# Layer 3 of a graph network: slots 1 to 11 as number pairs, blocks widened in five pieces, square roots placed later

## The chip, the cores and the metric

One NeuronCore of a Trainium2 chip runs the whole kernel. The metric is the device time of one execution in microseconds. TensorE multiplies, VectorE and ScalarE compute on vectors, GpSimd issues the gathers (indirect DMAs, which fetch rows by index), and SyncE issues the plain DMAs, of which ScalarE issues some too.

## The reference

Three graph convolutions over 6250 nodes and 106250 edges (100000 drawn ones, sorted by destination, and one self loop a node), then a residual and a layer norm:

```python
src = jnp.concatenate([edge_index[0], loops])
dst = jnp.concatenate([edge_index[1], loops])
deg = jax.ops.segment_sum(jnp.ones_like(dst, dtype=x.dtype), dst, num_segments=n)
dinv = jnp.where(deg > 0, jax.lax.rsqrt(deg), 0.0)
norm_edge = dinv[src] * dinv[dst]
for W, b in ((W1, b1), (W2, b2), (W3, b3)):
    h_in = h @ W
    agg = jax.ops.segment_sum(h_in[src] * norm_edge[:, None], dst, num_segments=n)
    h = jax.nn.relu(agg + b)
x = _layernorm(x + h, axis=-1)
```

Widths are 256 in, 512 hidden twice, 256 out. All is float32.

## The kernel before

The nodes are 49 tiles of 128. A layer's table (one row per node, already scaled by `dinv`) lies in DRAM, and each tile of the output is the sum of the rows that its edges name. The kernel has two ways to form such a sum, and layer 3 (`phase == 2`, from about 1900 us of the span on) uses both side by side.

**Gathered tiles.** The first 21 tiles (`GATHER`) of layer 3 take one *window* each. A window has up to 18 *slots*; a slot is 128 edges: GpSimd gathers their 128 source rows (L779), VectorE makes a 0/1 matrix `sel` from the destinations (L999, slots 0 to 8 "front" and 9 to 17 "back"), and TensorE multiplies the two into a PSUM sum. The window's sums alternate between `ps_acc` and `ps_d`. In layer 3 slots 1 to 8 (`PAIRED`) are fetched as *number pairs*: `table_pairs` holds each row as a high and a low part of type fp32r, 512 numbers or 2 KB, and TensorE multiplies `sel_r` with each part (L1743, two instructions of 256 columns). The other slots are fetched as single rows of 256 float32 numbers, 1 KB, and multiplied as float32 (L1747, which the trace shows as two instructions as well). Slots 0 and 9 to 17 are of that kind.

Rows are fetched into the place of the same slot of the window before. So GpSimd waits: slots 1 to 11 of window v are gathered as their groups were used in window v-1 (`slots_used`), and slots 12 to 15, and 16 and 17 where the tile needs them, after slot 0 of window v has been multiplied (`opened`), which shows that window v-1 is over.

**Dense tiles.** For the last 28 tiles (`DENSE`) the kernel has built matrices of counts earlier, 49 *blocks* of 128 by 128 to a tile, and stored them in DRAM, in bytes (`built_bytes`) or for ten of the tiles in bf16 (`built`). TensorE multiplies each block with the high and low parts of a source tile (L1850, 512 columns, fp32r), into `ps_T` and `ps_h` in turn. Before that, ScalarE *widens* the blocks to fp32r (L1526) from the loaded tile into one of two ring buffers, in pieces of 13 or 12 blocks (`PIECES`), 1664 or 1536 columns. After each piece ScalarE issues the load of the same piece of the tile after next (L1515). A widening waits until TensorE has finished the piece two before it (`dense_piece`), since it overwrites that ring buffer, and for the loaded tile (`blocks_in`).

**How they are interleaved.** Three windows and four dense tiles make a *group*; there are seven. TensorE's program is written out by hand: over the 54 slot positions of a group its 196 dense products are spread evenly, three or four of them ahead of each slot. Pieces are numbered 0 to 15 within a group, and four pieces are one tile.

**The square roots.** The layer norm of a finished tile runs on VectorE up to the variance (`mv`, L1100); ScalarE then takes the square root (`deviation`, L1534, which waits for `var_ready`), and VectorE goes on. ScalarE runs in order, so where `group` places a `deviation` among the widenings decides which piece waits behind it. A gathered tile is finished after its window's end: VectorE adds the sum (L1089), makes the next window's back half of `sel` and only then norms the tile. The names are `of_gather(g, b)` for window b and `of_dense(g, d)` for dense tile d of group g.

Of the kernel before, what the change touches and what calls it, by code (L numbers as in the profile page):

```python
# [30 lines left out]
P = 128  # L31
SLOTS = 18
FRONT = 9
PAIRED = range(1, FRONT)
GROUPS = [range(0, 1), range(1, 3), range(3, 6), range(6, 9), range(9, 12), range(12, 15), range(15, 16), range(16, 18)]
SURE = 16

STAY = 12
USED = 4
ORDER = [*range(0, SURE - 1), *range(SURE, SLOTS), SURE - 1]  # L40
# [21 lines left out]

PIECES = [(0, 13), (13, 25), (25, 37), (37, 49)]
LN_EPS = 1e-5


def gnn_program(nc, x, src, dst, W1, b1, W2, b2, W3, b3, out):
# [52 lines left out]
    with ctx:  # L120
# [52 lines left out]
        pair_rows = pair_rows_r.bitcast(F32)  # L173
        RING, RING_AT = PIECES[0][1], SINGLE + SLOTS * C
        ring = [rows_r[:, RING_AT + b * RING * P:RING_AT + (b + 1) * RING * P].rearrange("p (h d) -> p h d", d=P) for b in range(2)]
        assert PAIRED[0] == 1 and C + len(PAIRED) * 2 * C == SINGLE + (PAIRED[-1] + 1) * C and 2 * C == HID
        assert RING_AT + 2 * RING * P <= SLOTS * HID + COLS and all(hi_h - lo_h <= RING for lo_h, hi_h in PIECES)
        post = sb("post", [P, 2 * HID])
# [706 lines left out]
        def _(v_):  # L885
# [185 lines left out]
            def prepare_early(n, part, paired, to=sel):  # L1071

                if part == 0:
                    v_.wait_ge(slots_used, n * USED - 1)
                else:
                    v_.wait_ge(window_done, n)
                k = part * FRONT
                if paired and part == 0:
                    to = sel_r
                v.tensor_tensor(to[:, k:k + FRONT, :], numbers.unsqueeze(1).broadcast_to([P, FRONT, P]),  # L1080
                                early_dst[:, k:k + FRONT].unsqueeze(2).broadcast_to([P, FRONT, P]),
                                ALU.is_equal).then_inc((front_ready, back_ready)[part], 1)
# [28 lines left out]
            def finish_dense(g, d):  # L1111
                j, into, seq = DENSE_OF * g + d, d % 2, of_dense(g, d)
                v_.wait_ge(dense_piece, len(PIECES) * (j + 1))
# [65 lines left out]
            def one_window():  # L1179
                def steady(phase, t, odd, hots=None, whole=None, units=None, last=False, in_parts=False, tile=None, next_tile=None, dense=None):  # L1180
# [17 lines left out]
                    elif phase < 2:  # L1198
                        v.tensor_copy(idx[:, 1 - odd, :], early_src[:, :]).then_inc(idx_ready, 1)
                    prepare(n, t, base, 1, sel_parts if in_parts else sel)  # L1200
                    if phase == 1 and t > 1:
# [157 lines left out]
        def _(act):  # L1359
# [146 lines left out]
            def piece_in(j, into, piece):  # L1506

                lo_h, hi_h = PIECES[piece]
                its = blocks[into][:, lo_h:hi_h, :].rearrange("p h d -> p (h d)")
                return its.bitcast(U8)[:, 0:(hi_h - lo_h) * P] if in_bytes(j) else its  # L1510

            def load_blocks(j, into, piece):
                lo_h, hi_h = PIECES[piece]
                its = built_bytes if in_bytes(j) else built
                act.dma_start(piece_in(j, into, piece), its[j * P:(j + 1) * P, lo_h * P:hi_h * P]).then_inc(blocks_in[into], 16)  # L1515

            def widen(g, x, more=True):

                d, piece = divmod(x, len(PIECES))
                lo_h, hi_h = PIECES[piece]  # L1520
                whole_x = DENSE_OF * len(PIECES) * g + x
                act.wait_ge(blocks_in[d % 2], 16 * len(PIECES) * (DENSE_OF // 2 * g + d // 2 + 1))
                if not (isinstance(g, int) and whole_x < 2):
                    act.wait_ge(dense_piece, whole_x - 1)
                act.sem_inc(act_step, 1)
                nc.scalar.activation(ring[piece % 2][:, 0:hi_h - lo_h, :].rearrange("p h d -> p (h d)"),  # L1526
                                     piece_in(DENSE_OF * g + d, d % 2, piece), ACT.Copy).then_inc(widened, 1)
                if more:
                    act.wait_ge(widened, whole_x + 1)
                    load_blocks(DENSE_OF * g + d + 2, d % 2, piece)  # L1530
# [5 lines left out]
            def one_window():  # L1536
# [73 lines left out]
                act.wait_ge(tile_stored[1], 16 * len(PIECES) * (DENSE_1 // 2 + 2))  # L1610
                for piece in range(len(PIECES)):
                    load_blocks(0, 0, piece)
# [7 lines left out]
                for of in range(2):  # L1620
                    act.wait_ge(tile_stored[of], 16 * len(PIECES) * (DENSE // 2 + 1))
                for piece in range(len(PIECES)):
                    load_blocks(1, 1, piece)

                def group(g, first=False, last=False):

                    def pieces(*xs):
                        for x in xs:
                            widen(g, x, not (last and x >= 2 * len(PIECES)))

                    if not first:
                        deviation(of_gather(g - 1, 2))
                    if not first:
                        pieces(1)
                        deviation(of_dense(g - 1, 3))
                    pieces(2, 3, 4, 5)
                    deviation(of_dense(g, 0))
                    pieces(6)
                    deviation(of_gather(g, 0))
                    pieces(7, 8, 9)  # L1640
                    deviation(of_dense(g, 1))
# [31 lines left out]
        def _(pe):  # L1673
# [66 lines left out]
            def add_slot(to, phase, k, first, in_parts, start, stop):  # L1740
# [96 lines left out]
            def dense(g, d, h, first):  # L1837

                into = d % 2
                if h == 0:  # L1840
                    pe.wait_ge(dense_taken, DENSE_OF * g + d + 1)
                for piece, (lo_h, hi_h) in enumerate(PIECES):
                    if lo_h <= h < hi_h:
                        if h == lo_h:
                            pe.wait_ge(widened, len(PIECES) * (DENSE_OF * g + d) + piece + 1)
                        counts_of = ring[piece % 2][:, h - lo_h, :]
                        end = h == hi_h - 1
# [218 lines left out]
```

## Time and profile before

| | |
|---|---|
| time, median of 3 runs | 2373.16 us (2372.32 to 2376.5) |
| profiled execution: time | 2371.75 us |
| its span | 2369.9 us |
| TensorE busy | 2157.9 us, 91% of the span |
| GpSimd busy | 1696.4 us, 72% |
| VectorE, ScalarE busy | 866.9 us and 731.2 us |
| granted TensorE clock, mean | 0.978 |

The chain of work that ended last lies on TensorE for 56% of the span and on GpSimd for 14%. Times inside the trace are counted from the span's start. Shares over the whole span mix three layers with different limits; the change touches layer 3 alone.

### The profile page before, as it was taken

How to read it: one execution, taken by the hardware profiler on the slowest of the kernel's cores; microseconds unless marked ns; L12 is line 12 of the kernel's file. 1: busy time of each engine (PE TensorE's matmuls, PEld its weight loads, DVE VectorE, ACT ScalarE, POOL GpSimd, SP SyncE). 2: the span in 40 equal slices, each digit the busy share in tenths (PEclk: the TensorE clock that was granted, in tenths of full speed). 3: DMA queues.
4: the chain of work that ended last, by engine and by line, in shares of the span. 5: the costliest groups of instructions: out<-in, count | busy, mean ns of one | idle time of the engine just before them, and what ended most of it. 6: DMA issues, size and time to landing. Idle time of an engine off the chain costs nothing.

```text
span 2369.9 us, 33254 instructions
## 1 busy us (share of the span) xinstructions
PE 2157.9 (91%) x10765; PEld 1432.8 (60%) x10765; DVE 866.9 (37%) x1213; ACT 731.2 (31%) x1550; POOL 1696.4 (72%) x1768
## 2 busy tenths in 40 slices
PE   5777889999999998899998999989999899999998
PEld 4755567777777774444444444444444378888886
DVE  8887222222222212232333333333222334434333
ACT  7611223323333311232332323222231143443333
POOL 4277777777777766777777777777777777776774
PEclk9798999999999999999999999999999999999999
DMA  7446667677776766888887888888888787778884
GB/s 226 147 122 204 205 205 209 210 208 211 209 210 206 211 199 192 256 257 263 258 258 245 257 265 257 253 247 264 263 258 271 231 247 241 229 224 269 284 276 129
DMA packets 232394, 543.61 MB, mean 229 GB/s; under 512 B 39228, under 2 KB 107699, under 8 KB 232259
## 3 DMA queue, kind: packets, MB, share of 16 engines
q0 software_dynamic: 122592, 387.10, 55.1%
q1 hardware_dynamic: 91011, 121.92, 15.0%
q10 hardware_dynamic: 18656, 32.75, 4.3%
q8 instruction: 89, 1.46, 0.3%
q14 instruction: 46, 0.38, 0.1%
HBM read 455.62 MB, written 86.00 MB: 229 GB/s over the span
## 4 chain that ended last, share of the span: by engine, by line
PE 56%; POOL 14%; issue 13%; DMA 8%; DVE 7%; ACT 1%; POOLq 1%; ACTq 0%; DVEq 0%
POOL rows L779 14%; PE ps_o L1811 8%; PE ps_acc L1755 7%; PE ps_d L1755 7%; PE ps_h L1850 7%; DMA rows<-table,idx 7%; PE ps_d L1861 6%; PE ps_acc L1751 6%; PE ps_T L1850 5%; PE ps_h L1800 2%; PE ps_acc L1747 2%; PE ps_d L1747 2%; DVE big L942 1%; DMA rows<-table_parts,idx 1%; PE ps_e L1832 1%
## 5 line engine op out<-in xcount | busy, mean ns | idle before, releaser
L779 POOL DMA_INDIRECT rows<-table,idx x1081 | 1046.5, 968 | 374.9 <-issue 305.5
L1755 PE MATMUL ps_acc<-rows,sel 128*128 128x512 f32 (+2 forms) x1122 | 490.8, 566 | 81.1 <-DMA rows<-table,idx 58.6
L779 POOL DMA_INDIRECT rows<-table_parts,idx x483 | 456.6, 945 | 149.4 <-issue 139.5
L999 DVE SCALAR_TENSOR_TENSOR sel<-ps_e,firsts,dstT 128x1152 f32<-128x1152 f32 (+1 forms) x194 | 274.3, 1414 | 615.3 <-PE ps_acc L1755 209.1
L1755 PE MATMUL ps_d<-rows,sel 128*128 128x512 f32 (+1 forms) x850 | 411.3, 607 | 41.3 <-DMA rows<-table,idx 41.2
L1755 PEld LDWEIGHTS ps_acc<-rows,sel 128*128 128x128 f32 x1122 | 205.6, 201 | 231.2 <-issue 152.9
L1811 PE MATMUL ps_o<-low,hT 128*128 128x512 f32 (+1 forms) x784 | 272.2, 491 | 0.5 <-ACT hT L1433 0.5
L1751 PE MATMUL ps_acc<-rows,sel 128*128 128x256 bf16 (+1 forms) x1533 | 242.0, 274 | 23.1 <-DMA rows<-table_parts,idx 13.1
L1755 PEld LDWEIGHTS ps_d<-rows,sel 128*128 128x128 f32 x850 | 147.4, 191 | 178.5 <-issue 126.2
L1861 PE MATMUL ps_d<-big 128*128 128x256 bf16 x1470 | 226.6, 273 | 4.0 <-issue 3.6
L1850 PE MATMUL ps_T<-pairs_r,rows_r 128*128 128x512 f32 x686 | 210.1, 424 | 8.0 <-ACT rows_r L1526 8.0
L1811 PEld LDWEIGHTS ps_o<-low,hT 128*128 128x128 f32 x784 | 148.2, 193 | 104.9 <-issue 94.6
L1526 ACT ACTIVATE rows_r<-low 128x1664 fp32r<-128x1664 uint8 (+3 forms) x112 | 169.1, 1510 | 130.4 <-PE ps_h L1850 43.6
L1089 DVE TENSOR_TENSOR acc<-ps_acc,acc 128x256 f32<-128x256 f32 (+1 forms) x74 | 37.8, 511 | 464.0 <-PE ps_acc L1751 257.8
L1850 PE MATMUL ps_h<-pairs_r,rows_r 128*128 128x512 f32 x686 | 204.8, 418 | 2.6 <-ACT rows_r L1526 2.6
L779 POOL DMA_INDIRECT rows_r<-table_pairs,idx x168 | 159.0, 947 | 52.6 <-issue 48.7
L1454 ACT ACTIVATE big<-ps_o,dinv 128x256 f32<-128x256 f32 x49 | 23.2, 473 | 552.9 <-PE ps_o L1811 552.9
L1751 PEld LDWEIGHTS ps_acc<-rows,sel 128*128 128x128 bf16 x1533 | 148.2, 98 | 53.6 <-issue 17.9
L1861 PEld LDWEIGHTS ps_d<-big 128*128 128x128 bf16 x1470 | 140.2, 97 | 37.9 <-issue 25.6
L1850 PEld LDWEIGHTS ps_T<-pairs_r,rows_r 128*128 128x128 f32 x686 | 123.7, 189 | 29.9 <-ACT rows_r L1526 10.6
L1502 ACT ACTIVATE big<-ps_l 128x392 uint8<-128x392 f32 (+1 forms) x224 | 112.2, 501 | 95.2 <-PE ps_l L1832 94.9
L1850 PEld LDWEIGHTS ps_h<-pairs_r,rows_r 128*128 128x128 f32 x686 | 123.5, 189 | 25.0 <-issue 5.4
(215 smaller groups left out, 2084.0 us busy)
## 6 DMA issues: line engine op xcount, KB each, us to landing
rows<-table,idx POOLq DMA_INDIRECT x1081, 4.3
table<-made SPq DMA_DIRECT2D x49, 256.0 KB
acc<-table SPq DMA_DIRECT2D x49, 256.0 KB
table_pairs<-made_r SPq DMA_DIRECT2D x49, 256.0 KB, 4.3
built<-big SPq DMA_DIRECT2D x30, 384.0 KB
low<-built ACTq DMA_DIRECT2D x30, 384.0 KB, 4.8
built_bytes<-big SPq DMA_DIRECT2D x54, 192.0 KB
low<-built_bytes ACTq DMA_DIRECT2D x54, 192.0 KB, 3.9
```

What stands on the lines that cost most here:

```text
L779: pool.indirect_dma_start(out=to, out_offset=None, in_=its[0:nodes, :], in_offset=bass.IndirectOffsetOnAxis(ap=idx[:, of, k:k + 1], axis=0 ...
L999: v.scalar_tensor_tensor(to[:, k:k + FRONT, :], numbers.unsqueeze(1).broadcast_to([P, FRONT, P]), firsts[:, bass.ds(t, 1)], dstT[:, bass.d ...
L1089: v.tensor_tensor(acc[:, 0:w], ps[:, 0:w], acc[:, 0:w], ALU.add).then_inc(sum_taken, 1)
L1502: nc.scalar.activation(to[:, :, at:at + 2 * QUAD].rearrange("p h (b d) -> p h b d", b=2), built_banks[g % 2][:, 0:2 * QUADS].rearrange("p ...
L1526: nc.scalar.activation(ring[piece % 2][:, 0:hi_h - lo_h, :].rearrange("p h d -> p (h d)"), piece_in(DENSE_OF * g + d, d % 2, piece), ACT.C ...
L1747: return mm(to[:, 0:C], its, rows_3[:, k, :] if first is None else first, start=start, stop=stop)
L1751: ins = mm(to[:, 0:C], sel_parts[:, k, :], row[:, i * C:(i + 1) * C], start=start and i == 0, stop=stop and i == PARTS - 1)
L1755: return mm(to[:, 0:w], sel[:, k, :], rows_of[phase][:, k, 0:w] if first is None else first, start=start, stop=stop)
L1800: ins = mm(ps_h[:, m * P:(m + 1) * P], w1[:, k, m * P:(m + 1) * P], of[:, k * P:(k + 1) * P], start=(k == 0), stop=(k == KC - 1))
L1811: ins = mm(ps_o[:, 0:w], hT[:, m * P:(m + 1) * P], wt[:, m, :], start=(m == 0), stop=(m == KH - 1))
L1850: ins = mm(ps_dense[into].rearrange("p (i c) -> p i c", i=2), counts_of, pairs_r[:, :, h, :], start=(h == 0), stop=(h == T - 1))
L1861: ins = mm(ps_dense_1, making[of][:, h, :], parts[:, h, i, :], start=(h == 0 and i == 0), stop=(h == T - 1 and i == PARTS - 1))
```

## The change

It edits three things in layer 3. Slots 9, 10 and 11 are fetched and multiplied as number pairs too (`PAIRED` now ends at `STAY`, 12), and both halves of `sel` are made as `sel_r`. The widenings go by `RING_PIECES`, five pieces of 10, 10, 10, 10 and 9 blocks to a tile (1280 or 1152 columns), so that a group has 20 pieces; the ring index follows the running number of the piece, since five is odd. And `group` places the square roots elsewhere in the new order. The core of the diff:

```diff
-PAIRED = range(1, FRONT)
...
 STAY = 12
+PAIRED = range(1, STAY)
...
 PIECES = [(0, 13), (13, 25), (25, 37), (37, 49)]
+RING_PIECES = [(0, 10), (10, 20), (20, 30), (30, 40), (40, 49)]
...
-                if paired and part == 0:
+                if paired:
                     to = sel_r
...
-                    prepare(n, t, base, 1, sel_parts if in_parts else sel)
+                    prepare(n, t, base, 1, sel_parts if in_parts else sel_r if phase == 2 else sel)
...
-                nc.scalar.activation(ring[piece % 2][:, 0:hi_h - lo_h, :].rearrange("p h d -> p (h d)"),
+                nc.scalar.activation(ring[x % 2][:, 0:hi_h - lo_h, :].rearrange("p h d -> p (h d)"),
                                      piece_in(DENSE_OF * g + d, d % 2, piece), ACT.Copy).then_inc(widened, 1)
...
+                    if not first:
+                        pieces(1)
+                    pieces(2)
                     if not first:
                         deviation(of_gather(g - 1, 2))
+                    pieces(3)
                     if not first:
-                        pieces(1)
                         deviation(of_dense(g - 1, 3))
-                    pieces(2, 3, 4, 5)
+                    pieces(4, 5, 6)
                     deviation(of_dense(g, 0))
-                    pieces(6)
+                    pieces(7, 8)
                     deviation(of_gather(g, 0))
-                    pieces(7, 8, 9)
+                    pieces(9, 10, 11)
                     deviation(of_dense(g, 1))
-                    pieces(10, 11)
+                    pieces(12, 13, 14, 15)
                     deviation(of_gather(g, 1))
-                    pieces(12, 13, 14)
+                    pieces(16, 17, 18)
                     deviation(of_dense(g, 2))
-                    pieces(15)
+                    pieces(19)
...
                 if in_parts and phase == 2:
-                    its = sel_r[:, k, :].bitcast(F32) if k < FRONT else sel[:, k, :]
-                    return mm(to[:, 0:C], its, rows_3[:, k, :] if first is None else first, start=start, stop=stop)
+                    return mm(to[:, 0:C], sel_r[:, k, :].bitcast(F32), rows_3[:, k, :] if first is None else first, start=start, stop=stop)
...
-                        counts_of = ring[piece % 2][:, h - lo_h, :]
+                        counts_of = ring[(len(RING_PIECES) * d + piece) % 2][:, h - lo_h, :]
```

Everywhere else in layer 3 `PIECES` becomes `RING_PIECES`; the storing of the built blocks keeps the four old pieces. The number of instructions of GpSimd and VectorE does not change. Lines move by one to four: in the changed kernel L1747 is the product with a number pair (L1743 before), L1750 that with a single row (L1747 before), L1853 the dense product, L1527 the widening and L1535 the square root.

**ScalarE, the turn from group 0 to group 1.** `rows_r<-low` is a widening, `low<-built_bytes` the load behind it, `sd<-mv,eps` a square root. Before, from the widening of the new group's piece 0 on:

```order
L1526 ACTIVATE rows_r<-low 128x1664 [waits blocks_in0,dense_piece]
L1515 DMA low<-built_bytes 128x1664 [waits widened]
L1534 ACTIVATE sd<-mv,eps 128x1 [waits var_ready]
L1526 ACTIVATE rows_r<-low 128x1536 [waits blocks_in0,dense_piece]
L1515 DMA low<-built_bytes 128x1536 [waits widened]
L1534 ACTIVATE sd<-mv,eps 128x1 [waits var_ready]
L1526 ACTIVATE rows_r<-low 128x1536 [waits blocks_in0,dense_piece]
L1515 DMA low<-built_bytes 128x1536 [waits widened]
```

And now, from the same widening on:

```order
L1527 ACTIVATE rows_r<-low 128x1280 [waits blocks_in0,dense_piece]
L1516 DMA low<-built_bytes 128x1280 [waits widened]
L1527 ACTIVATE rows_r<-low 128x1280 [waits blocks_in0,dense_piece]
L1516 DMA low<-built_bytes 128x1280 [waits widened]
L1527 ACTIVATE rows_r<-low 128x1280 [waits blocks_in0,dense_piece]
L1516 DMA low<-built_bytes 128x1280 [waits widened]
L1535 ACTIVATE sd<-mv,eps 128x1 [waits var_ready]
L1527 ACTIVATE rows_r<-low 128x1280 [waits blocks_in0,dense_piece]
L1516 DMA low<-built_bytes 128x1280 [waits widened]
L1535 ACTIVATE sd<-mv,eps 128x1 [waits var_ready]
L1527 ACTIVATE rows_r<-low 128x1152 [waits blocks_in0,dense_piece]
L1516 DMA low<-built_bytes 128x1152 [waits widened]
```

The root of the last gathered tile stood ahead of piece 1 and now stands behind piece 2; the root of the last dense tile stood ahead of piece 2 and now stands behind piece 3.

**ScalarE, block 3 of group 0.** Before, the root of window 1's tile stands directly ahead of the first piece (1664 columns) of the fourth dense tile:

```order
L1526 ACTIVATE rows_r<-low 128x1536 [waits blocks_in0,dense_piece]
L1515 DMA low<-built_bytes 128x1536 [waits widened]
L1534 ACTIVATE sd<-mv,eps 128x1 [waits var_ready]
L1526 ACTIVATE rows_r<-low 128x1664 [waits blocks_in1,dense_piece]
L1515 DMA low<-built_bytes 128x1664 [waits widened]
```

Now, from the last piece (1152 columns) of the third dense tile on:

```order
L1527 ACTIVATE rows_r<-low 128x1152 [waits blocks_in0,dense_piece]
L1516 DMA low<-built_bytes 128x1152 [waits widened]
L1527 ACTIVATE rows_r<-low 128x1280 [waits blocks_in1,dense_piece]
L1516 DMA low<-built_bytes 128x1280 [waits widened]
L1535 ACTIVATE sd<-mv,eps 128x1 [waits var_ready]
L1527 ACTIVATE rows_r<-low 128x1280 [waits blocks_in1,dense_piece]
L1516 DMA low<-built_bytes 128x1280 [waits widened]
L1527 ACTIVATE rows_r<-low 128x1280 [waits blocks_in1,dense_piece]
```

The first piece of the fourth dense tile now comes ahead of that root, and its second piece behind it.

**TensorE, slots 9 and 10 of a window.** The rows are those of a steady window of layer 3, from the first of dense tile 2 (`ps_T`) on. Before:

```order
L1850 MATMUL ps_T<-pairs_r,rows_r 128x512 [waits widened,dense_taken]
L1850 MATMUL ps_T<-pairs_r,rows_r 128x512 x2
L1747 MATMUL ps_acc<-rows,sel 128x256 [waits back_ready,landed4]
L1850 MATMUL ps_T<-pairs_r,rows_r 128x512 x4
L1747 MATMUL ps_acc<-rows,sel 128x256
L1850 MATMUL ps_T<-pairs_r,rows_r 128x512 x3
```

And now:

```order
L1853 MATMUL ps_T<-pairs_r,rows_r 128x512 [waits widened,dense_taken]
L1853 MATMUL ps_T<-pairs_r,rows_r 128x512 x2
L1747 MATMUL ps_acc<-rows_r,sel_r 128x256 [waits back_ready,landed4]
L1747 MATMUL ps_acc<-rows_r,sel_r 128x256
L1853 MATMUL ps_T<-pairs_r,rows_r 128x512 x4
L1747 MATMUL ps_acc<-rows_r,sel_r 128x256 x2
L1853 MATMUL ps_T<-pairs_r,rows_r 128x512 x3
L1747 MATMUL ps_acc<-rows_r,sel_r 128x256 x2
```

Slots 9, 10 and 11 turn from `rows,sel` to `rows_r,sel_r`, with two products each where the order shows one; the dense products between them stay.

## Rows read from the trace of the kernel before

**Rows 1.** The windows view: 18 windows of layer 3, and the six with bf16 blocks.

```profile
core 0: us, PE busy (x) PEld busy (x) DVE busy (x) ACT busy (x) POOL busy (x), PEclk, DMA share, GB/s
1950.00:2340.00 390.00, 379.71 (x1793) 315.81 (x1792) 155.69 (x350) 154.45 (x138) 276.45 (x291) 1.00 0.80 250
2145.00:2275.00 130.00, 126.56 (x598) 105.27 (x597) 51.70 (x118) 51.50 (x46) 91.71 (x97) 1.00 0.85 278
```

**Rows 2.** The waits view of the same stretch: TensorE's waits, and GpSimd's for TensorE.

```profile
POOL rows L779 <- PE ps_d L1747: 15.3, 8, 3.3
...
POOL rows L779 <- PE ps_acc L1747: 14.6, 8, 2.6
...
PE ps_T L1850 <- ACT rows_r L1526: 8.0, 6, 1.3
...
PE ps_h L1850 <- ACT rows_r L1526: 2.3, 6, 0.4
```

**Rows 3.** The timeline of TensorE: start us, us, instruction, [idle before <-releaser].

```profile
2147.81 0.47 PE L1850 MATMUL ps_h<-pairs_r,rows_r 128*128 128x512 f32 x1 [0.38 <-ACT rows_r L1526]
...
2163.41 0.59 PE L1747 MATMUL ps_d<-rows,sel 128*128 128x256 f32 x2
2163.65 1.05 PE L1850 MATMUL ps_T<-pairs_r,rows_r 128*128 128x512 f32 x3
...
2169.26 0.50 PE L1850 MATMUL ps_T<-pairs_r,rows_r 128*128 128x512 f32 x1 [1.33 <-ACT rows_r L1526]
...
2180.86 0.40 PE L1850 MATMUL ps_h<-pairs_r,rows_r 128*128 128x512 f32 x1
...
2195.57 0.40 PE L1743 MATMUL ps_d<-rows_r,sel_r 128*128 128x256 f32 x2
```

**Rows 4.** The timeline of ScalarE in the same stretch.

```profile
2145.88 0.29 ACT L1534 ACTIVATE sd<-mv,eps 128x1 f32<-128x1 f32 x1 [4.41 <-DVE mv L1100]
2146.08 1.58 ACT L1526 ACTIVATE rows_r<-low 128x1664 fp32r<-128x1664 uint8 x1
...
2167.54 0.30 ACT L1534 ACTIVATE sd<-mv,eps 128x1 f32<-128x1 f32 x1 [5.90 <-DVE mv L1100]
2167.74 1.47 ACT L1526 ACTIVATE rows_r<-low 128x1536 fp32r<-128x1536 uint8 x1
...
2170.92 0.29 ACT L1534 ACTIVATE sd<-mv,eps 128x1 f32<-128x1 f32 x1 [1.71 <-DVE mv L1100]
...
2181.14 1.49 ACT L1526 ACTIVATE rows_r<-low 128x1536 fp32r<-128x1536 bf16 x1 [2.49 <-PE ps_T L1850]
...
2199.72 0.29 ACT L1534 ACTIVATE sd<-mv,eps 128x1 f32<-128x1 f32 x1 [2.38 <-DVE mv L1100]
```

**Rows 5.** The timeline of VectorE a variance.

```profile
2167.33 0.18 DVE L1100 BATCH_NORM_AGGREGATE mv<-stats 128x2 f32<-128x6 f32 x1
```

**Rows 6.** The chain that ended last, in order of time: start us, us, what.

```profile
2346.47 0.93 PE ps_h L1850 x4
2347.40 0.24 PE ps_acc L1743 x2
...
2348.33 0.43 PE ps_acc L1747 x2
```

**Rows 7.** The timeline of GpSimd, which issues the gathers.

```profile
1939.09 0.95 POOL L779 DMA_INDIRECT rows_r<-table_pairs,idx  x1 [0.30 <-issue]
...
1953.09 0.95 POOL L779 DMA_INDIRECT rows<-table,idx  x1 [0.30 <-issue]
...
1988.14 0.95 POOL L779 DMA_INDIRECT rows<-table,idx  x1 [0.30 <-issue]
```

**Rows 8.** The timeline of TensorE: slot 0 of the third window.

```profile
1948.77 0.59 PE L1747 MATMUL ps_acc<-rows,sel_r 128*128 x2
```

**Rows 9.** The DMA view of 2145 to 2275 us: queue of the gathers (packets, MB, share), and landing.

```profile
q0 software_dynamic: 6106, 18.79, 45.4%
...
rows<-table,idx POOLq DMA_INDIRECT x49, 4.4
```

More of the change, by code:

```diff
@@ L173, in gnn_program @@
         pair_rows = pair_rows_r.bitcast(F32)
-        RING, RING_AT = PIECES[0][1], SINGLE + SLOTS * C
+        RING, RING_AT = RING_PIECES[0][1], SINGLE + SLOTS * C
         ring = [rows_r[:, RING_AT + b * RING * P:RING_AT + (b + 1) * RING * P].rearrange("p (h d) -> p h d", d=P) for b in range(2)]
         assert PAIRED[0] == 1 and C + len(PAIRED) * 2 * C == SINGLE + (PAIRED[-1] + 1) * C and 2 * C == HID
-        assert RING_AT + 2 * RING * P <= SLOTS * HID + COLS and all(hi_h - lo_h <= RING for lo_h, hi_h in PIECES)
+        assert RING_AT + 2 * RING * P <= SLOTS * HID + COLS and all(hi_h - lo_h <= RING for lo_h, hi_h in RING_PIECES)
         post = sb("post", [P, 2 * HID])
@@ L1112, in finish_dense @@
                 j, into, seq = DENSE_OF * g + d, d % 2, of_dense(g, d)
-                v_.wait_ge(dense_piece, len(PIECES) * (j + 1))
+                v_.wait_ge(dense_piece, len(RING_PIECES) * (j + 1))
                 v.scalar_tensor_tensor(y1[:, :], ps_dense[into][:, 0:C], dinv[:, bass.ds(GATHER + j, 1)], b3b[:, :], ALU.mult, ALU.add).then_inc(y_d_scaled, 1)
@@ L1506, in piece_in @@
             def piece_in(j, into, piece):
-                lo_h, hi_h = PIECES[piece]
+                lo_h, hi_h = RING_PIECES[piece]
                 its = blocks[into][:, lo_h:hi_h, :].rearrange("p h d -> p (h d)")
@@ L1512, in load_blocks @@
             def load_blocks(j, into, piece):
-                lo_h, hi_h = PIECES[piece]
+                lo_h, hi_h = RING_PIECES[piece]
                 its = built_bytes if in_bytes(j) else built
@@ L1517, in widen @@
             def widen(g, x, more=True):
[L1519 to L1522, printed above, removed]
+                d, piece = divmod(x, len(RING_PIECES))
+                lo_h, hi_h = RING_PIECES[piece]
+                whole_x = DENSE_OF * len(RING_PIECES) * g + x
+                act.wait_ge(blocks_in[d % 2], 16 * len(RING_PIECES) * (DENSE_OF // 2 * g + d // 2 + 1))
                 if not (isinstance(g, int) and whole_x < 2):
@@ L1610, in one_window @@
                 act.wait_ge(tile_stored[1], 16 * len(PIECES) * (DENSE_1 // 2 + 2))
-                for piece in range(len(PIECES)):
+                for piece in range(len(RING_PIECES)):
                     load_blocks(0, 0, piece)
@@ L1621, in one_window @@
                     act.wait_ge(tile_stored[of], 16 * len(PIECES) * (DENSE // 2 + 1))
-                for piece in range(len(PIECES)):
+                for piece in range(len(RING_PIECES)):
                     load_blocks(1, 1, piece)
@@ L1628, in pieces @@
                         for x in xs:
-                            widen(g, x, not (last and x >= 2 * len(PIECES)))
+                            widen(g, x, not (last and x >= 2 * len(RING_PIECES)))
+                    if not first:
+                        pieces(1)
+                    pieces(2)
                     if not first:
                         deviation(of_gather(g - 1, 2))
+                    pieces(3)
                     if not first:
-                        pieces(1)
                         deviation(of_dense(g - 1, 3))
-                    pieces(2, 3, 4, 5)
+                    pieces(4, 5, 6)
                     deviation(of_dense(g, 0))
-                    pieces(6)
+                    pieces(7, 8)
                     deviation(of_gather(g, 0))
-                    pieces(7, 8, 9)
+                    pieces(9, 10, 11)
                     deviation(of_dense(g, 1))
-                    pieces(10, 11)
+                    pieces(12, 13, 14, 15)
                     deviation(of_gather(g, 1))
-                    pieces(12, 13, 14)
+                    pieces(16, 17, 18)
                     deviation(of_dense(g, 2))
-                    pieces(15)
+                    pieces(19)
                     if not last:
@@ L1841, in dense @@
                     pe.wait_ge(dense_taken, DENSE_OF * g + d + 1)
-                for piece, (lo_h, hi_h) in enumerate(PIECES):
+                for piece, (lo_h, hi_h) in enumerate(RING_PIECES):
                     if lo_h <= h < hi_h:
                         if h == lo_h:
-                            pe.wait_ge(widened, len(PIECES) * (DENSE_OF * g + d) + piece + 1)
-                        counts_of = ring[piece % 2][:, h - lo_h, :]
+                            pe.wait_ge(widened, len(RING_PIECES) * (DENSE_OF * g + d) + piece + 1)
+                        counts_of = ring[(len(RING_PIECES) * d + piece) % 2][:, h - lo_h, :]
                         end = h == hi_h - 1
```

## The prediction

> **What bounds the kernel now.** I read the busy shares by stretch first, because the change touches layer 3 alone and the page's shares mix three layers. In 1950 to 2340 us, which is 18 windows at 21.67 us each, TensorE is busy for 379.71 of 390 us and idle for 10.3, at a full granted clock [rows 1]. GpSimd is second: 276.45 us of gathers by this view. Then the waits of the same stretch: TensorE has only two groups of them, 8.0 us in six waits of up to 1.3 and 2.3 us in six of up to 0.4, both for ScalarE's widening (L1526) [rows 2]. Together that is 10.3 us, so all of TensorE's idle time is this one dependency, and no gather (a wait for a landing) is in it. Layer 3 is thus bound by TensorE's own work, plus ScalarE's lateness at two fixed places of each group.
>
> The timelines name the places. At 2169.26 TensorE starts again after 1.33 us [rows 3]; ScalarE had stood before the square root of 2167.54 (idle 5.90 us, released by `mv`), and its widening ran from 2167.74 to 2169.21 [rows 4]. That is piece 1 of a group behind the root of the previous group's last gathered tile. At 2147.81 it is 0.38 us [rows 3], and the widening of 1664 columns ran from 2146.08 to 2147.66, behind the root of 2145.88 [rows 4]: piece 12 behind window 1's root. Both roots wait for a variance which VectorE can only have some 4 us after the window's last slot: slot 17 is multiplied at 2163.41 [rows 3], `mv` is ready at 2167.33 + 0.18 = 2167.51 [rows 5]. The widening itself was allowed much earlier, since TensorE had finished the piece two before it at 2163.65 [rows 3].
>
> **The change, part by part.**
>
> *Three slots as pairs.* In the chain, a pair slot takes 0.24 us of TensorE, a single one 0.43, and four dense products 0.93 [rows 6]. (The chain shows 0.23 and 0.24 for pair slots; I take 0.235.) Slots 9, 10 and 11 of each of 21 windows change kind: 63 x 0.195 = 12.3 us less. Nothing hides this: TensorE is the busy engine there and the slots lie in line with the dense products. Bounds: 63 x 0.19 = 12.0 and 63 x 0.20 = 12.6 by the rounding of these rows.
>
> One rule bears on this term. By the Trainium skill, FP8 and Floating Point Precision, section TensorE Precision Notes, a true float32 product takes four passes of the array where reduced precision takes one; if so, a single slot would be twice a pair slot, 0.47 us, and by that the term would be 63 x 0.235 = 14.8 us, an estimate from that page. The row shows 0.43, and the sum goes by the row.
>
> *The roots later.* The walk goes by rows of the steady group. ScalarE starts a widening 0.28 us after TensorE has gone on to the next piece (2180.86 to 2181.14) [rows 3, 4]. A widening costs 1.58 us for 1664 columns and 1.47 to 1.49 for 1536 [rows 4], so about 0.10 us for 128 columns, and 1.28 for 1280. A root holds the queue 0.20 us (2167.54 to 2167.74) [rows 4].
> - Group start, at t = 0 = 2163.65. Piece 1 may start at 0.28 and ends by 1.6; TensorE needs it after 10 dense products, t = 3.2 (10 x 0.232 + one single + two pair slots). Piece 2 may start at 3.5 and ends at 4.8, needed at 6.2. The gathered tile's variance is there at 3.9, so its root starts at 4.8 without waiting. The dense tile's root follows 3.4 us behind (2167.54 to 2170.92) [rows 4], so at 8.2. Piece 3 runs from 6.5 to 7.8, and piece 4 may start only at 9.6. Neither root holds a widening up: 1.33 us falls away, and nothing new comes.
> - Window 1's end. The root's variance is 4.1 us behind the last slot (2163.41 to 2167.51). The widening behind it is now piece 16, which must wait for the end of piece 14: from that last slot on two single slots, three pair slots, 16 dense products and the 0.28, 5.6 us. The root is over by 4.5. The 0.38 us falls away.
> - The tightest new place is the root of dense tile 1, ahead of piece 12. It came 4.15 us after slot 8's product (2195.57 to 2199.72) [rows 3, 4], as VectorE makes a front half first. Piece 12 may start 3.3 us after that slot, so the root delays it by some 1.0 us: it ends at 4.35 + 1.28 = 5.6. TensorE needs it after 20 dense products, three pair and two single slots: 6.2. That leaves 0.6 us. The other places leave 0.9 or more by the same walk.
>
> So all twelve waits of the stretch go; with the short one at the end of the last group (0.3 us, outside the stretch) that is 10.3 + 0.3 = 10.6 us. Bounds: 10.6 if every place holds, and 10.6 - 7 x 0.5 = 7.1 if the tightest place is 1.1 us worse than I walk it.
>
> *Five pieces.* Per tile ScalarE pays one more fixed part, 1.49 - 12 x 0.10 = about 0.3 us, and one more load to issue. It is busy for 154 of 390 us [rows 1], and its cover is the 3.1 us that TensorE spends on a piece of ten against 1.28 of widening and the 0.5 around it. Cost nothing; if the cover were gone, each late widening would show as a wait like the two above. The ring is refilled by shorter steps, so the margin of a step falls from about 2.0 to 1.3 us.
>
> *VectorE* makes the same matrices into the other type: nothing.
>
> *GpSimd* issues the same number of gathers. It is the next engine in line. Its pitch while it waits for nothing: 39 steps from 1939.09 to 1988.14, 1.258 us each [rows 7]. 291 gathers in the 18 windows [rows 1] need 366 us. The other way: it waited for TensorE 15.3 + 14.6 = 29.9 us in 16 waits [rows 2], of which 0.3 each is its usual gap, so 25.1 us is real slack and 365 us is needed. TensorE will need 379.7 - 54 x 0.195 = 369.2 us. GpSimd stays under by 3 to 4 us in 18 windows, 0.2 a window. That is thin, and the source of my second case. The start matters too, as GpSimd is behind then: slot 12 of the third window is gathered at 1953.09 [rows 7], 4.3 us after that window's slot 0 at 1948.77 [rows 8]. With TensorE 1.2 us earlier there the lag is 5.5; slots 12 to 14 are awaited together, so the third is issued 2.5 us later and lands 4.4 after its issue [rows 9]: 12.4 us, needed at 13.2 (44 dense products, one single and eleven pair slots). It holds by 0.8 us.
>
> *The DMA engines.* Each window fetches 3 x 128 KB more. The gathers' queue moved 18.79 MB in 45.4% of 130 us [rows 9], 3.14 us a MB. In the stretch with bf16 blocks, share 0.85 [rows 1], that is 110.5 + 2.36 x 3.14 = 117.9 us of engine time in 130 - 3.5 - 3.4 = 123.1 us: 96%. Over the 18 windows: 312 + 22 = 334 in 369, 91%. Rows land a window ahead of their use for slots 1 to 11, so I cost it at nothing; between nothing and what rival 3 gives.
>
> A rule of the Trainium skill speaks against the change here: DMA: Bandwidth & Descriptors, section Issuing engines are not separate DMA queues, says that transfers of all issuing engines share the same 16 DMA engines. The same page (Where 436 GB/s comes from) gives a core some 358 GB/s from HBM; 278 GB/s [rows 1] would become 314, an estimate of 88% by that figure. Neither gives another sum.
>
> **The sum.** 12.3 + 10.6 = 22.9 us. The profiled execution took 2371.75 us: 2348.9. It lies 1.4 us under the median of 2373.16, so the predicted time is 2350.
>
> **The rivals.**
> 1. *GpSimd becomes the bound.* For: 0.2 us a window of margin. Against: the 39 steps above are as they ran beside dense loads and other traffic, at a DMA share near 0.8. If the pitch rose to 1.29 with the larger gathers, 291 of them need 375 us, 6 more than TensorE: 2356; at 1.30, 2359.
> 2. *The roots only move the wait.* If the walk is wrong at the tightest place by 1.1 us, 0.5 us a group comes back: 2353.5. If both old waits reappear in full elsewhere, only the slots' 12.3 us are left: 2361.
> 3. *Slower than before.* The mechanism is the DMA engines: if the doubled rows make landings so late that TensorE waits in every window. It would decide once a window takes 21.8 us instead of 20.5 (22.9 + 4.7 us over 21 windows). The engine time in a window would be 334 / 18 = 18.6 us on average, and 19.7 with bf16 blocks; it would have to be 17% higher. Against it: even at twice the cost for each added MB it is 19.8. At that point the time is 2378.
> 4. *The pairs do nothing.* Only if the slots' time were hidden; TensorE's 97% in the stretch [rows 1] excludes it.
>
> **How the numbers follow.** Forecast as summed: 0.65, own range 2347 to 2353.5. GpSimd: 0.14 (2353 to 2360). Waits that come back: 0.12 (2353 to 2361). Slower or a tie through the DMA engines: 0.05. Something that I don't see: 0.04. The range from 2347 to 2359 leaves out some 0.17. This kernel's runs tell 0.2%, 4.7 us, from no change. Faster by more: 0.93; within: 0.04; slower: 0.03.
>
> **What would show it.** Right: windows of 20.5 us in the steady part; no wait of TensorE for `rows_r` in layer 3; GpSimd's wait for slot 0's product down from 25 us to a few in all; the slots 9 to 11 at 0.24 us in the chain; DMA share near 0.9. Wrong: GpSimd without a wait and TensorE waiting for landings, above all of slots 12 to 14; or a wait for `rows_r` ahead of piece 12.

## The result, and the profile after

The changed kernel takes 2347.03 us (median of 4 runs, 2344.51 to 2347.62), the kernel before beside it 2373.09 us (2372.32 to 2376.5). The ratio is 0.9885, with a 95% interval of 0.9868 to 0.9903. That is 26.1 us less, where the sum forecast 22.9: faster by the two parts that were forecast and at the places that were forecast, but by more. By the medians the time lies on the lower bound of the forecast's own range, 2347; by the ratio, applied to the 2373.16 of before, it is 2345.9 and below it. The profiled execution took 2347.62 us, 24.1 less than the one before.

The windows view of the changed kernel: 350 us of layer 3, up to some 35 us before TensorE's last product, and the stretch with bf16 blocks.

```profile
1950.00:2300.00 350.00, 350.00 (x1715) 295.51 (x1714) 151.20 (x338) 155.59 (x156) 264.46 (x279) 1.00 0.89 290
2145.00:2275.00 130.00, 130.00 (x634) 109.69 (x633) 53.97 (x122) 58.03 (x58) 98.04 (x104) 1.00 0.94 318
```

TensorE was idle for 10.3 of 390 us in layer 3 [rows 1] and is now idle for nothing in 350 us. The waits view of 1950 to 2340 us has no row of TensorE either. It has these of GpSimd, which waited 29.9 us in 16 waits for TensorE before [rows 2]:

```profile
POOL rows L780 <- issue: 29.1, 92, 0.7
...
POOL rows_r L780 <- PE ps_acc L1747: 1.5, 5, 0.3
POOL rows_r L780 <- PE ps_d L1747: 1.2, 4, 0.3
POOL rows_r L780 <- PE ps_acc L1750: 0.6, 2, 0.3
POOL rows L780 <- PE ps_acc L1747: 0.6, 2, 0.3
POOL rows_r L780 <- PE ps_d L1750: 0.6, 2, 0.3
```

The usual gap between two gathers is 0.3 us, so these fifteen waits are no more than that. From the second window on only four gaps of GpSimd stand out, of 0.49 to 0.71, about 1 us in all beyond the usual 0.3. It works through with almost no rest.

The chain, to be held against [rows 6]. Line 1750 is a single row's slot, line 1747 a pair's.

```profile
2301.60 0.93 PE ps_h L1853 x4
2302.53 0.24 PE ps_d L1747 x2
...
2307.87 0.43 PE ps_d L1750 x2
```

The window's eleven pair slots now take 0.23 or 0.24 us each; the costs of one slot are as before, and only the kind of three has changed.

The timeline of ScalarE at the turn from group 3 to group 4, where [rows 4] had the widening of 2167.74 behind a root:

```profile
2151.62 1.27 ACT L1527 ACTIVATE rows_r<-low 128x1280 fp32r<-128x1280 uint8 x1 [1.21 <-PE ps_h L1853]
...
2155.05 1.27 ACT L1527 ACTIVATE rows_r<-low 128x1280 fp32r<-128x1280 uint8 x1 [2.16 <-DMA low<-built]
...
2156.74 0.29 ACT L1535 ACTIVATE sd<-mv,eps 128x1 f32<-128x1 f32 x1 [0.42 <-ACT rows_r L1527]
2158.08 1.27 ACT L1527 ACTIVATE rows_r<-low 128x1280 fp32r<-128x1280 uint8 x1 [1.04 <-PE ps_T L1853]
...
2160.28 0.29 ACT L1535 ACTIVATE sd<-mv,eps 128x1 f32<-128x1 f32 x1 [0.93 <-DVE mv L1101]
2161.10 1.17 ACT L1527 ACTIVATE rows_r<-low 128x1152 fp32r<-128x1152 uint8 x1 [0.53 <-DMA low<-built]
```

The first row is piece 1, which no longer has a root ahead of it. The first root's variance is now ready before the queue gets to it: the row after piece 2 shows no wait for `mv`.

### The profile page after: what moved, and what is told of

It reads as the page before. It is cut to its first block, busy times and chain, and to the rows that moved or that the text cites. A ratio compares the mean times of both kernels' runs of the same rounds, so it can differ in the third digit from the quotient of the medians.

```text
span 2345.9 us, 33339 instructions
## 1 busy us (share of the span) xinstructions
PE 2149.1 (92%) x10765; PEld 1428.3 (61%) x10765; DVE 867.6 (37%) x1213; ACT 739.6 (32%) x1578; POOL 1694.6 (72%) x1768
## 4 chain that ended last, share of the span: by engine, by line
PE 59%; POOL 14%; issue 13%; DMA 7%; DVE 6%; POOLq 1%; ACTq 0%; DVEq 0%; ACT 0%
POOL rows L780 14%; PE ps_acc L1758 8%; PE ps_o L1814 7%; PE ps_T L1853 7%; PE ps_h L1853 7%; PE ps_d L1758 6%; PE ps_acc L1754 6%; PE ps_d L1864 6%; DMA rows<-table,idx 6%; PE ps_h L1803 3%; DVE big L943 1%; PE ps_acc L1747 1%; PE ps_acc L1750 1%; PE ps_d L1750 1%; PE ps_d L1747 1%
## 5 line engine op out<-in xcount | busy, mean ns | idle before, releaser
L780 POOL DMA_INDIRECT rows<-table,idx x1018 | 984.5, 967 | 331.5 <-issue 293.8
L1000 DVE SCALAR_TENSOR_TENSOR sel<-ps_e,firsts,dstT 128x1152 f32<-128x1152 f32 (+1 forms) x174 | 246.0, 1414 | 615.8 <-PE ps_acc L1758 209.9
L780 POOL DMA_INDIRECT rows_r<-table_pairs,idx x231 | 219.4, 950 | 72.9 <-issue 68.7
L1527 ACT ACTIVATE rows_r<-low 128x1280 fp32r<-128x1280 uint8 (+3 forms) x140 | 175.3, 1252 | 186.8 <-PE ps_h L1853 83.2
L1853 PE MATMUL ps_T<-pairs_r,rows_r 128*128 128x512 f32 x686 | 200.7, 411 | 0.0
L1853 PE MATMUL ps_h<-pairs_r,rows_r 128*128 128x512 f32 x686 | 200.1, 411 | 0.0
L1853 PEld LDWEIGHTS ps_h<-pairs_r,rows_r 128*128 128x128 f32 x686 | 121.9, 189 | 18.6
L1503 ACT ACTIVATE big<-ps_e 128x392 uint8<-128x392 f32 (+1 forms) x224 | 111.8, 499 | 68.0 <-PE ps_e L1835 61.0
```

The costliest lines, as they stand in the source:

```text
L780: pool.indirect_dma_start(out=to, out_offset=None, in_=its[0:nodes, :], in_offset=bass.IndirectOffsetOnAxis(ap=idx[:, of, k:k + 1], axis=0 ...
L1000: v.scalar_tensor_tensor(to[:, k:k + FRONT, :], numbers.unsqueeze(1).broadcast_to([P, FRONT, P]), firsts[:, bass.ds(t, 1)], dstT[:, bass.d ...
L1503: nc.scalar.activation(to[:, :, at:at + 2 * QUAD].rearrange("p h (b d) -> p h b d", b=2), built_banks[g % 2][:, 0:2 * QUADS].rearrange("p ...
L1527: nc.scalar.activation(ring[x % 2][:, 0:hi_h - lo_h, :].rearrange("p h d -> p (h d)"), piece_in(DENSE_OF * g + d, d % 2, piece), ACT.Copy) ...
L1853: ins = mm(ps_dense[into].rearrange("p (i c) -> p i c", i=2), counts_of, pairs_r[:, :, h, :], start=(h == 0), stop=(h == T - 1))
```

## The experiments

In their measurements "PE waits" are those of the waits view of layer 3. Window lengths are the distances between slot 0's products. The kernel before was run again beside each batch: its median was 2373.26 us beside runs 1 to 4, 2373.41 beside runs 5 to 7 and 2373.09 beside the changed kernel. Differences of two medians are taken to be good to 1 or 2 us; window lengths, which mostly repeat to 0.02 us, are the finer measure.

**Run 1, the roots alone.** From the kernel before, with its four pieces and eight pair slots:

```diff
                     if not first:
+                        pieces(1)
                         deviation(of_gather(g - 1, 2))
+                    pieces(2)
                     if not first:
-                        pieces(1)
                         deviation(of_dense(g - 1, 3))
-                    pieces(2, 3, 4, 5)
+                    pieces(3, 4, 5)
...
-                    pieces(10, 11)
+                    pieces(10, 11, 12)
                     deviation(of_gather(g, 1))
-                    pieces(12, 13, 14)
+                    pieces(13, 14)
```

> The kernel before with the roots placed later among the four pieces a tile (behind pieces 1, 2, 12 in place of ahead of them); no new pairs, no five pieces. Theory A (a wait of TensorE for a widening costs its idle time and some 0.26 us more, which the profile counts as busy): 13 waits go, 10.6 + 3.4 = 14.0 us, 2359.1. Theory B (the waits cost their idle time alone and the three slots are worth 15.5 us): 10.6 us, 2362.5. Theory C (the five pieces are needed for it): about 2371.

Measured: 2359.16 us (2356.76 to 2359.59), ratio 0.9938 [0.9922, 0.9955], no PE wait. That is 14.1 us less, though the waits of before show only 10.6 of idle time. The moved roots are worth more than the waits view says, by 3.5 us.

The rows of slot 0 in the timeline of TensorE, in the kernel before, for a window without a wait, one with the short and one with the long wait:

```profile
1927.72 0.59 PE L1747 MATMUL ps_d<-rows,sel_r 128*128 x2
...
1970.20 0.59 PE L1747 MATMUL ps_d<-rows,sel_r 128*128 x2
...
1992.20 0.59 PE L1747 MATMUL ps_acc<-rows,sel_r 128*128 x2
```

With [rows 8] between the first two these are windows of 21.05, 21.43 and 22.00 us. In run 1 the same three are:

```profile
1926.75 0.59 PE L1748 MATMUL ps_d<-rows,sel_r 128*128 x2
1947.80 0.59 PE L1748 MATMUL ps_acc<-rows,sel_r 128*128 x2
1968.61 0.59 PE L1748 MATMUL ps_d<-rows,sel_r 128*128 x2
1989.00 0.59 PE L1748 MATMUL ps_acc<-rows,sel_r 128*128 x2
```

That is 21.05, 20.81 and 20.39. So a short wait costs 0.62 us where the rows say 0.38 idle, and a long one 1.61 where they say 1.33.

**Run 2, five pieces alone,** roots where they were, slots 9 to 11 single:

```diff
-PAIRED = range(1, STAY)
+PAIRED = range(1, FRONT)
...
                     if not first:
+                        deviation(of_gather(g - 1, 2))
                         pieces(1)
-                    pieces(2)
-                    if not first:
-                        deviation(of_gather(g - 1, 2))
-                    pieces(3)
-                    if not first:
                         deviation(of_dense(g - 1, 3))
-                    pieces(4, 5, 6)
+                    pieces(2, 3, 4, 5, 6)
...
-                    pieces(12, 13, 14, 15)
+                    pieces(12, 13, 14)
                     deviation(of_gather(g, 1))
-                    pieces(16, 17, 18)
+                    pieces(15, 16, 17, 18)
```

> Slots 9 to 11 single as before, five pieces, roots at the old places (ahead of pieces 1, 2 and 15 of twenty). Theory A and B: piece 1 is due after 10 dense products and not 13, so the wait there grows from 1.3 to about 2.3 us a group; slower than the kernel before by 4 to 7 us, 2377 to 2380. Theory C (finer pieces help by themselves): 2365 or less.

Measured: 2379.29 us (2375.91 to 2381.5), ratio 1.0024 [1.0014, 1.0033]. The waits view has

```profile
PE ps_T L1850 <- ACT rows_r L1527: 11.2, 7, 1.8
```

Shorter pieces with the roots in the old places are slower than before. The margin of a step is smaller, so the same late root reaches TensorE as 1.82 us instead of 1.33. The time, 6.0 us over the kernel before, is as expected, but the idle time of a wait is not: 2.3 us were expected. The piece is due three products earlier (0.70 us) and its widening is 0.20 us shorter (1.27 in place of 1.47), which makes 1.33 + 0.50 = 1.83. A window with this wait is 2.4 us longer than in run 1, or more: 1.82 idle, the 0.28 that went with a wait before, and 0.3 at the piece behind the second root, which comes late too and in five of six groups shows no idle time. The window at the old place of window 1's root is 0.3 us longer as well, with none shown. The last section says more of the windows that are longer still.

**Run 3, five pieces and the roots,** without the new pairs: the changed kernel with `PAIRED = range(1, FRONT)`.

> Slots 9 to 11 single as before, five pieces and the roots as in the changed kernel. Theory A: the same as four pieces with late roots, 2359.1; the changed kernel is then 12.3 us faster than this one by the three slots alone. Theory B: 2362.5, and the changed kernel 15.5 faster than it.

Measured: 2360.05 us (2357.89 to 2362.13), ratio 0.9944 [0.9928, 0.9961], no PE wait, and the window lengths of run 1. Run 3 against run 1 is the price of the fifth piece: nothing that can be told. The changed kernel against run 3 is the price of the slots: 13.0 us by the medians. By window, 19 windows of run 3 take 396.93 us and the same 19 of the changed kernel 385.40, so 0.61 us for three slots, 0.20 each and 12.7 in 21 windows. The forecast was 12.3 with bounds of 12.0 to 12.6.

**Run 4, the pairs with the roots in their old places:** the changed kernel with the edits of run 2 to the places of the roots, and `PAIRED` left as it is.

> The changed kernel with the roots at the old places. Theory A: 12.3 us under the run with five pieces, old root places and single slots, near 2366, windows with a wait of about 2.3 us at each group's start. Theory B: 15.5 us under it. If GpSimd already bounds the changed kernel, the difference between these two runs is larger than between the two with late roots.

Measured: 2367.79 us (2363.82 to 2372.08), ratio 0.9978 [0.9969, 0.9988], which is 11.5 under run 2, within the spread of theory A's 12.3. TensorE waits 11.3 us in seven waits, and still the slots' gain is there: where neither run's clock fell after a wait, a window is 0.59 to 0.61 us shorter than in run 2, but for two neighbours with 0.52 and 0.70. The two parts add up, because both lie on TensorE. Had GpSimd bound the changed kernel, this difference would be larger than the one with late roots, 13.0; it isn't.

This run shows the hidden part of a wait by itself. The timeline of TensorE early in the third window, where the piece behind the root of the second one's tile is due:

```profile
1951.79 0.63 PE L1849 MATMUL ps_T<-pairs_r,rows_r 128*128 128x512 f32 x2
1952.48 0.47 PE L1849 MATMUL ps_h<-pairs_r,rows_r 128*128 128x512 f32 x1
1952.79 0.40 PE L1743 MATMUL ps_acc<-rows_r,sel_r 128*128 128x256 f32 x2
```

and the same three in the changed kernel:

```profile
1953.69 0.63 PE L1853 MATMUL ps_T<-pairs_r,rows_r 128*128 128x512 f32 x2
1954.16 0.39 PE L1853 MATMUL ps_h<-pairs_r,rows_r 128*128 128x512 f32 x1
1954.39 0.40 PE L1747 MATMUL ps_acc<-rows_r,sel_r 128*128 128x256 f32 x2
```

From the first row to the third it is 1.00 us against 0.70. No idle time stands in brackets, and the waits view has no row for it; the window is 0.31 us longer all the same (1948.11 to 1968.62, against 1950.01 to 1970.21). ScalarE's row of the same place ends at 1952.33, about when the product could begin:

```profile
1951.08 1.25 ACT L1527 ACTIVATE rows_r<-low 128x1280 fp32r<-128x1280 uint8 x1
```

A lateness of about 0.3 us fits between the moment when the next product could start and the end that the profile models for the last one, so it is counted as busy.

**Run 5, one root moved back.** To have one wait a group in an otherwise changed kernel:

```diff
                     if not first:
+                        deviation(of_gather(g - 1, 2))
                         pieces(1)
                     pieces(2)
-                    if not first:
-                        deviation(of_gather(g - 1, 2))
                     pieces(3)
```

> The changed kernel with one root back at its old place: that of the last gathered tile ahead of piece 1, six times in all. Theory A: TensorE's idle by the waits view is near 1.8 us each, 10.8 in all, and the time lost is that and 0.26 a time, 10.8 + 1.6 = 12.4 us: 2359.5, with a window that holds a wait longer than its neighbours by 2.06 us. Theory B (idle time is the whole price): 2357.8, window longer by 1.8.

Measured: 2364.31 us (2361.64 to 2368.84), ratio 0.9962 [0.9949, 0.9976]: later than either theory. The waits view has

```profile
PE ps_T L1852 <- ACT rows_r L1527: 11.1, 6, 1.9
```

so 17.3 us of loss against the changed kernel for 11.1 us idle. Two of the six windows are near what theory A has, 2.13 us longer (1.88 idle and 0.25). The other four are 3.6 to 3.7 us longer, and the windows view says why. The first columns are the busy times of TensorE, its weight loads, VectorE, ScalarE and GpSimd; the third from the end is the granted clock.

```profile
2037.00:2039.00 2.00, 0.70 (x5) 0.41 (x3) 1.42 (x5) 0.91 (x2) 1.70 (x2) 1.00 0.75 231
2039.00:2041.00 2.00, 1.41 (x6) 1.18 (x7) 1.84 (x5) 1.49 (x2) 1.39 (x3) 0.87 0.85 237
2041.00:2043.00 2.00, 2.00 (x7) 1.61 (x7) 0.18 (x1) 0.33 (x1) 1.45 (x2) 0.50 0.82 215
2043.00:2045.00 2.00, 2.00 (x11) 1.73 (x10) 0.00 (x0) 0.68 (x1) 1.64 (x2) 0.77 0.77 240
```

The granted clock falls from 1.00 to 0.50 (2.4 to 1.2 GHz) about a microsecond after the wait of 1.89 us and comes back some 3.4 us later. The timeline of TensorE shows the price, four dense products at 2041.16 for 1.91 us and at 2044.51 for 1.09:

```profile
2039.59 1.34 PE L1852 MATMUL ps_T<-pairs_r,rows_r 128*128 128x512 f32 x4 [1.89 <-ACT rows_r L1527]
...
2041.16 1.91 PE L1852 MATMUL ps_T<-pairs_r,rows_r 128*128 128x512 f32 x4
...
2044.51 1.09 PE L1852 MATMUL ps_T<-pairs_r,rows_r 128*128 128x512 f32 x4
```

With 1.5 us for each of four such places and 2.13 for each of six waits the sum is 18.8; 17.3 were measured between the medians, and 19.1 between the two profiled executions from slot 0 of the second window on (1931.62 of 2367.1 us, and 1929.55 of 2345.9). The waits of 1.33 us in the kernel before were followed by a full clock:

```profile
2169.00:2171.00 2.00, 1.74 (x9) 1.52 (x10) 1.63 (x5) 0.29 (x2) 1.60 (x2) 1.00 0.80 178
2171.00:2173.00 2.00, 2.00 (x13) 1.69 (x12) 0.58 (x2) 1.59 (x2) 1.48 (x2) 1.00 0.82 268
```

**Run 6, larger rows without their use.** Slots 9 to 11 are fetched as pairs, but only the high part is multiplied, as float32, at the old 0.43 us. The low part is left out of the sum.

```diff
+                if in_parts and phase == 2 and FRONT <= k < STAY:
+                    return mm(to[:, 0:C], sel_r[:, k, :].bitcast(F32), pair_rows[:, k - PAIRED[0], 0:C], start=False, stop=False)
```

> The changed kernel, but slots 9 to 11 multiply the high part alone as float32 (the low part of those rows is fetched and left out of the sum). So the DMA engines move the larger rows and TensorE works as with single slots. If the larger rows cost nothing by themselves: the time of the run with five pieces, late roots and single slots, 2360 within 2. If the landings are later in a way that counts: above 2363, with waits of TensorE for a landing.

Measured: 2360.02 us (2358.33 to 2363.45), ratio 0.9947 [0.9927, 0.9966], and no PE wait: run 3's time. The windows view of 1950 to 2300 us of this run, and of run 3 under it (the DMA share is the last but one):

```profile
1950.00:2300.00 350.00, 350.00 (x1667) 294.05 (x1666) 145.04 (x326) 150.59 (x152) 256.46 (x270) 1.00 0.87 280
```

```profile
1950.00:2300.00 350.00, 350.00 (x1666) 293.75 (x1665) 144.46 (x326) 151.37 (x152) 256.29 (x269) 1.00 0.83 261
```

The added bytes raise the share by 0.04 and cost no time. The Trainium skill has the rule that speaks against it (DMA: Bandwidth & Descriptors, section Issuing engines are not separate DMA queues): all transfers run on the same 16 engines. The share of 0.87 fits that rule and leaves them room.

**Run 7, less dense work.** Four blocks of each dense tile are left out of the sums, 112 products or 26.0 us of TensorE:

```diff
-                            dense(g, d, h, first)
+                            if h not in (11, 21, 31, 41):
+                                dense(g, d, h, first)
```

> The changed kernel without 4 of the 49 dense products of each dense tile (blocks 11, 21, 31, 41 are left out of the sums), 112 products of 0.232 us, 26 us of TensorE's work. If TensorE alone bounded layer 3 the time would fall to about 2321. Theory: GpSimd's gathers are the next bound, at 319 gathers of 1.255 to 1.26 us for 20 windows, 20.05 us a window against 20.28 now; so only 3 to 5 us are gained, 2342 to 2344, and TensorE waits for landings.

Measured: 2343.36 us (2342.21 to 2343.71), ratio 0.9873 [0.9856, 0.989]. Of 26.0 us of work taken away the time gives back 3.7. From slot 0 of the second window to slot 0 of the last one a window takes 20.04 us on average, where 20.05 was expected from the gathers' pitch. TensorE now waits, and for landings:

```profile
PE ps_d L1747 <- DMA rows_r<-table_pairs,idx: 7.8, 8, 2.0
PE ps_acc L1747 <- DMA rows_r<-table_pairs,idx: 4.8, 8, 0.9
```

The last gather of the changed kernel, and of this run, in the timeline of GpSimd:

```profile
2321.36 0.95 POOL L780 DMA_INDIRECT rows<-table,idx  x1 [0.30 <-issue]
```

```profile
2321.75 0.95 POOL L780 DMA_INDIRECT rows<-table,idx  x1 [0.30 <-issue]
```

It is issued at nearly the same time (0.4 us later) with 26 us less of TensorE's work: the gathers are paced by GpSimd itself, in the changed kernel already. What the run gains lies behind the last gather.

## Why the prediction was nearly right, and where it fell short

*The slots.* Right to 0.4 us: 12.3 us were forecast from 0.43 and 0.235 a slot; the windows give 12.7, the medians 13.0. The rows of the changed kernel show 0.43 us for a single slot again, and 0.23 or 0.24 for a pair's. The estimate of 14.8 us, which the prediction worked out from the Trainium skill's rule of four passes (FP8 and Floating Point Precision, section TensorE Precision Notes), is too high: it took a single slot as exactly twice a pair's, and by the rows it is 1.83 times. No run here tells whether the rule or that step from it is off.

*The roots.* Right in mechanism and place. Every one of TensorE's 13 waits is gone, and run 1 shows it without the other edits. The walk held, but for piece 1. With t = 0 at 2151.59 in the changed kernel's trace, piece 1 starts at 0.03 us and not at 0.28: the prediction counted from the product behind slot 17, and the piece two before was done when slot 17 began, 0.24 us earlier. That erred on the safe side. Piece 2 starts at 3.5 us (forecast 3.5), the gathered tile's root at 5.2 (4.8), piece 3 at 6.5 (6.5), the dense tile's root at 8.7 (8.2) and piece 4 at 9.5 (9.6). At the tightest place, ahead of piece 12, the rows of ScalarE are

```profile
2185.46 0.29 ACT L1535 ACTIVATE sd<-mv,eps 128x1 f32<-128x1 f32 x1 [2.60 <-DVE mv L1101]
2185.66 1.26 ACT L1527 ACTIVATE rows_r<-low 128x1280 fp32r<-128x1280 bf16 x1
```

Slot 8's product was at 2181.31, so the root is 4.15 us behind it, as forecast, and the piece ends at 2186.92, 5.6 us behind it. TensorE shows no wait there.

*The step that failed* is the size of this term: "10.3 + 0.3 = 10.6 us. Bounds: 10.6 if every place holds". It took the idle time in the waits view for the whole price of a wait and for its upper bound. Run 1 measured 14.1 by the medians, and 13.35 over the twelve waits of its windows, where 10.3 were idle. The timeline of TensorE in the kernel before has, around the long wait of [rows 3]:

```profile
2167.07 0.87 PE L1850 MATMUL ps_T<-pairs_r,rows_r 128*128 128x512 f32 x3
...
2169.60 0.40 PE L1743 MATMUL ps_acc<-rows_r,sel_r 128*128 128x256 f32 x2
```

Three dense products began at 2167.07, so the next could go at 2167.77 (3 x 0.232); the profile lets them end at 2167.94. That hides 0.17 us. The first product after the wait of [rows 3], at 2169.26, took until 2169.60 to make room for the next instruction, 0.34 instead of 0.23: another 0.11. With 0.24 and 0.28 us by the two kinds of window, 13 waits hide some 3.4 us. 12.3 + 10.6 + 3.4 = 26.3 us, and 26.1 were measured; with 12.7 for the slots it would be 26.7, so the terms close to 0.6 us or better. Theory A, which was worked out from these rows after the result, was borne out by runs 1 and 4, whose times it gave beforehand. Theory B fell with run 1, 14.1 us and not 10.6, and with run 3, where the slots are worth 13 and not 15.5, and theory C fell with run 1, which has the full gain with four pieces.

The two profiled executions bear it out. From slot 0 of the second window to slot 0 of the last one, 19 windows on, it is 410.16 us before (1927.72 to 2337.88) and 385.40 after (1929.55 to 2314.95), 24.76 less; the prediction's terms give 21.4 for it (19 windows of 0.585 and the 10.3), and 12 waits of 0.26 more give 24.5. A window now takes 20.28 us on average, where the prediction's sign of being right was 20.5. From there to the span's end it is 1.07 us less. Ahead of it the changed kernel is 1.83 us behind, and its windows view has

```profile
1904.00:1906.00 2.00, 0.79 (x5) 0.79 (x6) 0.00 (x0) 1.91 (x4) 1.70 (x2) 0.96 0.73 217
1906.00:1908.00 2.00, 2.00 (x6) 1.56 (x6) 0.00 (x0) 1.27 (x1) 1.39 (x3) 0.50 0.72 189
```

The granted clock is 0.50 here at the start of layer 3, where it was 1.00 in the kernel before. The same program can do without: run 5's kernel has the same instructions up to this point, and its profile shows 1.00 from 1898 to 1922 us. It is no earlier for it, with slot 0 of the second window at 1931.62. Over all the profiles that slot lies between 1926.75 and 1931.62. Runs 4 and 6, with the larger gathers too, have a drop to 0.50 between 1902 and 1910 us, and runs 1 to 3, without them, have none there; run 7 has its own already at 1898 to 1900. Whether the gathers make it more frequent stays open.

*Five pieces.* Right: nothing (run 3 against run 1). They are not needed for the roots, which run 1 moves with four. They make room: the ring takes 20 blocks and not 26, and the larger rows of three more pair slots lie beside it, in the 768 numbers a partition that this frees. The new pairs with four pieces were not tried.

*The DMA engines.* Right: no time (run 6). The share of 0.94 in the bf16 stretch is near the 0.96 of the estimate, and the 318 GB/s near its 314. Other transfers do land later: the stores of finished tiles took 3.8 us in the median from issue to landing in 1950 to 2340 us, and 2.4 before; no wait of TensorE comes of it.

*GpSimd.* Right that it does not yet bound the kernel, but its margin was sized too large, by the same step. The prediction set 369.2 us of TensorE against 365 to 366 of GpSimd in 18 windows and had 3 to 4 us left. Take the hidden part of twelve waits, 3.1 us, off the 369.2 and 366.1 are left: no margin. Its real slack went from 25 us to about 1, and run 7 shows that it is level with TensorE now. So rival 1 is the next bound and was missed by little.

*VectorE* now waits up to 1.6 us for the later root at the turn of a group; nothing of TensorE waits for that.

## What to carry to other kernels

When an in-order engine feeds the busy one, place a step that must wait for something else behind as much of the feed as the margin allows, and walk each place with the times of its rows: that walk held here to within half a microsecond. Price a wait of TensorE by the length of a period with it and of one without it, not by the idle time ahead of the product, which was 0.24 to 0.28 us short at each wait here and shows none at all for a lateness of 0.3. And once the busy engine waits for nothing, see who is level with it before taking more of its work away: 26 us less brought 3.7.

## What the runs showed of the hardware

A wait of TensorE can cost more than its length. Of run 5's six waits of 1.82 to 1.89 us, four were followed by a granted clock of 0.50 for about 3.4 us and cost 3.6 to 3.7 us each instead of 2.1. None of the waits of 1.33 us in the kernel before was: all six of its windows with one are 1.6 us longer than in run 1. In run 5 the fall began 0.2 to 1.5 us after the wait's end. It is not the length alone that decides, since two waits of 1.88 us had no such drop and three of 1.82 had one. In run 2 two of the six windows with a wait of 1.82 us are 3.6 us longer than in run 1, with the clock at 0.50 after the wait, and the other four 2.4 to 2.7. In run 4 it is one of six. Together that is seven of eighteen waits of 1.82 to 1.89 us, and what decides between them was not tried.
